# A one-core attention and feed-forward kernel: a new opening for stage one, another look at the weights' low bits, and inverse roots by Newton steps

## The reference

```python
x = x + LN(attention(LN(x)))     # q, k, v = LN(x) @ W + b; causal softmax((q k^T + bias) / sqrt(8)) v @ Wo + bo
x = x + LN(ffn(x))               # ffn is fed LN(x) too
# bias[i, j] = q_i . rel_key[clip(j - i + 255, 0, 255)]
# ffn: silu(x W1 s1) * (x W2 s2), then twice gelu(h H s), then (h W3) s3; W1, W2, H1, H2, W3 ternary, hidden width 512
```

## Time and profile before

| | |
|---|---|
| median of three runs | 788.54 us |
| the profiled execution: its own time, its span | 789.45 us, 787.7 us |
| PE, PE weight load, DVE, ACT, POOL busy | 646.7, 470.4, 565.0, 562.4, 301.0 us |
| mean granted TensorE clock | 0.927 |
| first matmul of stage two, first of stage three | 137.37, 577.69 us |
| packets of 16 engines, moved | 41169, 52.79 MB |

### The profile page before, as it was taken

How to read it: one execution, slowest core, us unless ns; L and a number is a source line. 1 busy time by engine, 2 the same in 40 slices (tenths; PEclk the granted TensorE clock), 3 DMA queues, 4 the chain that set the end, 5 groups by cost and what they waited for, 6 DMA issues and landing times. The chain is left out here.

```text
span 787.7 us, 19097 instructions
## 1 busy us (share of the span) xinstructions
PE 646.7 (82%) x8064; PEld 470.4 (60%) x8064; DVE 565.0 (72%) x927; ACT 562.4 (71%) x657; POOL 301.0 (38%) x190
## 2 busy tenths in 40 slices
PE   0667632679999999999999999987779899898993
PEld 0323310556767667676676766855568678687682
...
DMA packets 41169, 52.79 MB, mean 67 GB/s; under 512 B 7410, under 2 KB 31554, under 8 KB 38658
## 3 DMA queue, kind: packets, MB, share of 16 engines
...
...
## 5 line engine op out<-in xcount | busy, mean ns | idle before, releaser
L960 PE MATMUL p_s<-q_sb,k_sb 96*128 96x128 bf16 (+1 forms) x1600 | 170.8, 249 | 18.7 <-DVE probs L1106 14.9
L1224 ACT ACTIVATE probs<-p_s 128x1024 f32<-128x1024 f32 x160 | 156.8, 1018 | 17.8 <-DVE p_s L1115 10.8
L1224 ACT ACTIVATE probs<-probs 128x1024 f32<-128x1024 f32 x128 | 133.7, 1057 | 46.4 <-DVE probs L1106 46.2
L1004 PE MATMUL p_o<-probs,v_sb 128*32 128x128 f32 (+1 forms) x3200 | 159.1, 330 | 7.6 <-ACT o_acc L1242 5.3
L960 PEld LDWEIGHTS p_s<-q_sb,k_sb 96*128 96x128 bf16 x1600 | 112.7, 100 | 77.7 <-issue 29.0
L916 POOL TENSOR_SCALAR_AFFINE_SELECT even_b<-even_b 128x2048 f32<-128x2048 f32 x32 | 75.5, 2360 | 216.3 <-ACT even_b L1235 216.3
L1106 DVE TENSOR_TENSOR probs<-p_s,even_b 128x1024 f32<-128x1024 f32 x96 | 115.0, 1220 | 28.4 <-PE p_s L960 16.0
L1004 PEld LDWEIGHTS p_o<-probs,v_sb 128*32 128x32 f32 x3200 | 84.5, 111 | 40.7 <-issue 13.5
L1653 PE MATMUL p_z<-hid_hi,h_hi 128*128 128x512 f32 x256 | 102.3, 399 | 1.7 <-POOL hid_lo L1574 1.7
L1656 PE MATMUL p_z<-hid_lo,h_hi 128*128 128x512 f32 x256 | 100.8, 394 | 0.0
L981 PE MATMUL p_s<-q_rows,rel_w 72*128 72x64 bf16 x2048 | 84.8, 197 | 18.2 <-DVE probs L1106 8.7
...
## 6 DMA issues: line engine op xcount, KB each, us to landing
...
q_dram<-q_parts SPq DMA_DIRECT2D x12, 256.0 KB, 3.5
k_dram<-k_parts SPq DMA_DIRECT2D x12, 256.0 KB, 3.8
qr_dram<-q_turned SPq DMA_DIRECT2D x12, 256.0 KB, 3.5
...
every<-in_L_ffn_h_w_dram SPq DMA_DIRECT2D x2, 1024.0 KB, 8.3
```

Of the source, the lines that this page charges most:

```text
L960: last = nc.tensor.matmul(slot[:, c:c + n * BLK], k_sb[hg][:, h * S + j * BLK:h * S + (j + 1) * BLK], ap(q_sb[hg], at, [[HG * S, KROWS], [ ...
L1004: last = nc.tensor.matmul(p_o[32 * h:32 * h + 32, at:at + blocks * BLK], v_sb[hg][:, j, h * 32:(h + 1) * 32], probs[n % PBUFS][:, h, col * ...
L1224: nc.scalar.activation(to, got, ACT.Exp, scale=SCALE).then_inc(t_exp, 1)
```

## The change

Six things change. (1) SP loads the bias table as it lies (`rel_n`) and PE transposes it into `p_v`; the other small loads count on semaphores of their own, the three weights on `s_wts`; `kb_c` is computed behind the table's parts, and the wait for `g_ext` (`s_gld`) stands in the first batch. (2) GpSimd no longer fills the padding rows of `q_sb` and `k_sb`; it fills a tile `pads`, and SP copies that by four transfers, waits for them, and then loads the weights. (3) The root of batch 1 stands behind `kf` of batch 0 on ACT. (4) The look at the weights is three passes of ACT over the low 16 bits of each word, all at the end of the first batch; GpSimd has no part in it. (5) All inverse roots past stage one are Newton steps on DVE, in place of ACT's Sqrt and DVE's reciprocal. (6) In the last unit the outputs and the projection stand two steps earlier, DVE's `first_again` one, and GpSimd does the scaling of both norms.

```diff
+def inverse_root(nc, dve, x, room, done, at):
+    bits = mybir.dt.int32
+    t, y = room[:, :, 0], room[:, :, 1]
+    nc.vector.tensor_scalar(t.bitcast(bits), x[:, :].bitcast(bits), 1, None, ALU.logical_shift_right).then_inc(done, 1)
+    dve.wait_ge(done, at + 1)
+    nc.vector.tensor_scalar(y.bitcast(bits), t.bitcast(bits), -1.0, float(ROOT_GUESS), ALU.mult,
+                            ALU.add).then_inc(done, 1)
+    for i in range(ROOT_STEPS):
+        dve.wait_ge(done, at + 2 + 3 * i)
+        nc.vector.scalar_tensor_tensor(out=t, in0=y, scalar=-0.5, in1=x[:, :], op0=ALU.mult,
+                                       op1=ALU.mult).then_inc(done, 1)
+        dve.wait_ge(done, at + 3 + 3 * i)
+        nc.vector.tensor_tensor(t, t, y, ALU.mult).then_inc(done, 1)
+        dve.wait_ge(done, at + 4 + 3 * i)
+        nc.vector.scalar_tensor_tensor(out=y, in0=t, scalar=1.5, in1=y, op0=ALU.add,
+                                       op1=ALU.mult).then_inc(done, 1)
 def normalised(nc, dve, ffn, n, which, src):
 
-    at = n * PRE + 6 + 5 * which
-    dve.wait_ge(ffn.r_sd, n * 2 + which + 1)
-    nc.vector.reciprocal(ffn.rs[:, :], ffn.rs[:, :]).then_inc(ffn.r_dv, 1)
-    dve.wait_ge(ffn.r_dv, at)
+    at = (2 * n + which) * ROOT_OPS
+    inverse_root(nc, dve, ffn.rs, ffn.st, ffn.r_root, at)
+    dve.wait_ge(ffn.r_root, at + ROOT_OPS)
     for t in range(NB):
-        last = nc.vector.tensor_scalar(ffn.y[:, t, :], src[:, t, :], ffn.mv[:, t, 0:1], ffn.rs[:, t:t + 1],
+        last = nc.vector.tensor_scalar(ffn.y[:, t, :], src[:, t, :], ffn.mv[:, t, 0:1], ffn.st[:, t, 1:2],
                                        ALU.subtract, ALU.mult)
-    last.then_inc(ffn.r_dv, 1)
+    last.then_inc(ffn.r_dv, 2)
 
...
-                             (bq_c[:, :], bq.rearrange("(p a) -> p a", a=1)),
+            sp.dma_start(rel_n[:, :, :], ap(rel.tensor, 0, [[HD, 128], [128 * HD, P // 128], [1, HD]])).then_inc(s_relt, 16)
+            for dst, src in ((wq_sb[:, :], Wq), (wk_sb[:, :], Wk), (wv_sb[:, :], Wv)):
+                sp.dma_start(dst, src).then_inc(s_wts, 16)
+            for dst, src in ((bq_c[:, :], bq.rearrange("(p a) -> p a", a=1)),
                              (bk_c[:, :], bk.rearrange("(p a) -> p a", a=1)),
                              (r0_c[:, :], ap(rel.tensor, 0, [[0, H], [1, HD], [1, 1]])),
-                             (bv_b[:, :, :], ap(bv.tensor, 0, [[0, 128], [0, NB], [1, 128]])),
-                             (rel_t[:, :], ap(rel.tensor, 0, [[1, HD], [HD, P]]))):
+                             (bv_b[:, :, :], ap(bv.tensor, 0, [[0, 128], [0, NB], [1, 128]]))):
                 sp.dma_start(dst, src).then_inc(s_par, 16)
             sp.wait_ge(s_xin, 16)
             tokens(1)
...
+            sp.wait_ge(s_pool, 9)
+            for p in range(2):
+                for rows, dst, which in ((ROWS + PARTS, q_sb[p], 0), (ROWS, k_sb[p], 1)):
+                    n = KROWS - rows
+                    sp.dma_start(ap(dst, rows * (HG * S), [[HG * S, n], [512, HG * S // 512], [1, 512]]),
+                                 ap(pads, which * 512, [[2 * 512, n], [0, HG * S // 512], [1, 512]])).then_inc(s_pads, 16)
+            sp.wait_ge(s_pads, 16 * 4)
...
+            nc.gpsimd.memset(pads[:, 0, :], 0.0)
+            step(nc.gpsimd.memset(pads[:, 1, :], 1.0), 9)
             for p in range(2):
-                step(nc.gpsimd.memset(q_sb[p][64:KROWS, :], 0.0), 9 + 4 * p)
-                step(nc.gpsimd.memset(k_sb[p][64:KROWS, :], 1.0), 10 + 4 * p)
                 pad = v_sb[p][:, :, :].rearrange("p n (h d) -> p n h d", h=HG)
...
-                if b == 0:
-                    remainder(0)
-                    remainder(1)
-            remainder(2)
...
                 dve.wait_ge(s_kx, b * KX + 2)
+                if first:
+                    dve.wait_ge(s_gld, 16)
                 nc.vector.tensor_tensor(k_ext[:, :], k_ext[:, :], g_ext[:, 0:2], ALU.add).then_inc(s_kx, 1)
...
             layernorm(0, True)
-            dve.wait_ge(s_par, 8 * 16)
-            nc.vector.tensor_tensor(kb_c[:, :], bk_c[:, :], r0_c[:, :], ALU.add).then_inc(s_gs, 1)
-            nc.vector.tensor_scalar(rel_s[:, :], rel_t[:, :], rel_t[:, 0:1], None, ALU.subtract).then_inc(s_gs, 1)
+            rel_t = p_v[0:HD, 0:P]
+            dve.wait_ge(s_gtr, 1)
+            nc.vector.tensor_copy(gx[:, 2:3], rel_t[:, 0:1]).then_inc(s_gs, 1)
+            dve.wait_ge(s_gs, 1)
+            nc.vector.tensor_scalar(rel_s[:, :], rel_t, gx[:, 2:3], None, ALU.subtract).then_inc(s_gs, 1)
             dve.wait_ge(s_gs, 2)
...
-            dve.wait_ge(s_gld, 16)
+            dve.wait_ge(s_par, 4 * 16)
+            nc.vector.tensor_tensor(kb_c[:, :], bk_c[:, :], r0_c[:, :], ALU.add).then_inc(s_gs, 1)
...
-            def rounded(i):
+            def low_bits(i):
                 act.wait_ge(s_every, 16 * len(WEIGHTS))
-                if i >= 2:
-                    act.wait_ge(s_wabs, i - 1)
-                got, part = checked(i)
-                nc.scalar.activation(part, got, ACT.Copy).then_inc(s_whi, 1)
-            def largest(i):
-                act.wait_ge(s_wlo, i + 1)
-                _, part = checked(i)
-                nc.scalar.activation(part, part.bitcast(F32), ACT.Abs, accum_out=low_max[:, i:i + 1]).then_inc(s_wabs, 1)
+                if i > 0:
+                    act.wait_ge(s_wabs, i)
+                n = every.shape[1]
+                c = slice(i * (HC * HID), min((i + 1) * (HC * HID), n))
+                low = every[:, c].bitcast(mybir.dt.uint16).rearrange("p (c two) -> p c two", two=2)[:, :, 0]
+                nc.scalar.activation(low_part[:, 0:c.stop - c.start], low, ACT.Copy,
+                                     accum_out=low_max[:, i:i + 1]).then_inc(s_wabs, 1)
 
             def batch(b, first, last_batch):
-                if last_batch:
-                    largest(0)
-                    rounded(2)
-                    largest(1)
-                if not last_batch:
+                if not first and not last_batch:
                     root(b + 1)
...
+                if first:
+                    root(1)
...
-                    rounded(0)
-                    rounded(1)
+                    for i in range(CHECKS):
+                        low_bits(i)
 
             root(0)
             transposed(0, True)
-            act.wait_ge(s_par, 8 * 16)
-            act.wait_ge(s_gs, 1)
+            act.wait_ge(s_par, 4 * 16)
+            act.wait_ge(s_gs, 10)
             batches(act, batch)
-            largest(2)
...
+            pe.wait_ge(s_relt, 16)
+            for x in range(P // 128):
+                last = nc.tensor.transpose(p_v[0:HD, x * 128:(x + 1) * 128], rel_n[:, x, :], ident[:, :])
+            last.then_inc(s_gtr, 1)
             transposes(0, True)
-            pe.wait_ge(s_par, 8 * 16)
+            pe.wait_ge(s_wts, 3 * 16)
             project_qk(0, True)
+            pe.wait_ge(s_gs, 2)
             project_v(0, True)
-            pe.wait_ge(s_gs, 10)
+            pe.wait_ge(s_gs, 11)
...
-    FFN_AT = {17: OUTPUTS, 20: PROJECT, 32: HIDDEN, STEPS: 3, STEPS + 1: 4, STEPS + 2: 5}
+    FFN_AT = {15: OUTPUTS, 18: PROJECT, 32: HIDDEN, STEPS: 3, STEPS + 1: 4, STEPS + 2: 5}
     PARTS_OF = {3: [(0, 0, 1), (1, 0, 1)], 4: [(2, 0, 2)], 5: [(2, 2, 2)]}
-    ROOT_AT = {22: 0, 29: 1}
-    FIRST_AT = {21: 0, 23: 1, 28: 2, 30: 3}
+    FIRST_AT = {19: 0, 27: 1}
...
+            def scaled(which, src, steps):
+                pool.wait_ge(ffn.r_root, (which + 1) * ROOT_OPS)
+                pool.wait_ge(ffn.r_dv, 5 + 5 * which)
+                for t in range(NB):
+                    last = nc.gpsimd.tensor_scalar(ffn.y[:, t, :], src[:, t, :], ffn.mv[:, t, 0:1], ffn.st[:, t, 1:2],
+                                                   ALU.subtract, ALU.mult)
+                last.then_inc(ffn.r_dv, steps)
+            scaled(0, ffn.y, 2)
             pool.wait_ge(ffn.r_dv, 7)
             pool.wait_ge(ffn.r_x, 16)
             nc.gpsimd.tensor_tensor(ffn.x1_first[:, :, :], ffn.x1_first[:, :, :], ffn.y[:, :, :], ALU.add).then_inc(ffn.r_x1, 1)
+            scaled(1, ffn.x1_first, 2)
...
+                dve.wait_ge(ffn.r_dv, 5)
+                inverse_root(nc, dve, ffn.rs, ffn.st, ffn.r_root, 0)
 
             def first_again():
                 dve.wait_ge(ffn.r_x1, 1)
                 statistics(nc, dve, ffn.st, ffn.mv, ffn.rs, lambda t: ffn.x1_first[:, t, :], ffn.r_dv, 8, ffn.alone)
+                dve.wait_ge(ffn.r_dv, 10)
+                inverse_root(nc, dve, ffn.rs, ffn.st, ffn.r_root, ROOT_OPS)
 
             def first(k):
                 if k in FIRST_AT:
-                    (first_y, first_scale, first_again, first_hidden)[FIRST_AT[k]]()
+                    (first_y, first_again)[FIRST_AT[k]]()
...
-            def pre_root(n, which):
-                act.wait_ge(r_dv, n * PRE + (5, 10)[which])
-                nc.scalar.activation(ffn.rs[:, :], ffn.rs[:, :], ACT.Sqrt).then_inc(r_sd, 1)
-            def post_root(n):
```

(50 more changed lines are left out.)

20 lines of the change are left out of this document (4 added, 16 removed).

## The result

The changed kernel takes 798.87 us (median of 4 runs, 797.51 to 800.71), the kernel before on the same chip 788.63 (788.49 to 789.47): a ratio of 1.013, 95% interval 1.0115 to 1.0146. It is 10.2 us slower where 13.7 faster was forecast. The profiled executions span 797.8 and 787.7 us, 10.1 apart.

What follows compares the result with a forecast made beforehand. Stage one was taken as a chain of small steps with gaps, feed-forward turns as bound by TensorE with DVE nearly gapless. Terms -22.8 (stage one), -2.0 (last unit), +11.1 (turns) gave -13.7: 774.8 us against 788.54, range 770 to 779.

Steps and rivals of the forecast that it cites:

- Opening: Stage one up to batch 0's k_ext: 12.7 us gained; ends 14, or 8 if the small loads land late.
- Look at the weights: Stage one, batch 0 to 1: three ACT passes, 2.0 us gained; ends 3.5 gained and 3 lost.
- About 40.5, and ACT wants them at 39.9. I charge 0.5: Look at the weights: their landing about 40.5 against ACT's need at 39.9, charged 0.5 us.
- Rival C: Weights or wide-stride pass hold ACT, by pads' landing or passes of 11.8: 5.5 us more, 780.3; chance 0.14.
- Last batch and end: Last batch to the end of stage one: 8.1 us gained; ends 5.3 and 11.2.
- Last unit: Last attention unit, Newton chains for ACT's roots: about 2.0 us gained; ends 5 gained and 1 lost.
- The first of them ... 2.8 gained: Last unit: first ACT root leaves the chain to o_acc, where TensorE waits 4.24; 2.8 us gained.
- I take 2.8: Last unit: GpSimd's scaling of 8 operations, taken as 2.8 us; ends 1.0 and 4.
- Stage three: Feed-forward turns with Newton chains: 11.1 us lost (0, 3.6, 3.6, 3.9 by turn); ends 8 and 17.
- the sign I gave for the turn's end: Turns 1 and 2: TensorE idle again about 4 us on DVE act_f, where it read 1.09.
- rival D: TensorE's granted clock falls behind stalls of 3 to 4 us: 4 us more, 778.8; chance 0.10.
- Rivals A and B: A: Newton steps cost far more, 796 at 0.45 us each, chance 0.04. B: DVE has more air, 767.6, chance 0.14.

Runs made afterwards that it cites:

- e3: Changed kernel with bv_b's load on its own semaphore, issued behind the second batch's tokens; 797.94 us.
- e10: Changed kernel with bv_b loaded as 128 pieces in place of 1024 and read eight times by the value add; 793.77 us.
- e2: Changed kernel with the weights' loads issued ahead of the four pad copies, the wait for pads only before the last batch; 791.25 us.
- e12: Changed kernel with later roots as in the kernel before, bv_b as 128 pieces, weights behind tokens, pads behind the first batch's stores; 769.16 us.
- e4: Changed kernel with the last unit's two scalings on VectorE behind their Newton chains, in place of GpSimd; 793.88 us.
- e6: Changed kernel with weights ahead of pads, bv_b's own late wait, Newton roots only in the last unit, its scalings on VectorE; 772.06 us.
- e8: Changed kernel with five Newton steps in place of three; 815.42 us.

## Why the prediction was wrong, point by point

**Opening, 12.7 forecast, 8.9 got.** Rightly seen: the memsets, rel_t, the root behind kf. What failed is "Ends: 14 ... 8 if the small loads land late": I took the late landing for an end where it was the case. bv_b stood in the same list before, hidden since everything waited for the 24.30 of rel_t. e3 shows 23.33, so the chain's own sum (24.4) was right but for this load, and 1 us too long.

**Look at the weights, 2.0 forecast; 5.7 of the opening's gain lost.** This is the step that failed worst: 7.7 us, a third of the miss. "About 40.5, and ACT wants them at 39.9. I charge 0.5" fell in "pads to 25, waits to about 28.5": SP issued the last pad at 31.3 and waited to 39.2. Of the 10.7 us by which the weights were issued late (39.2 for 28.5), 6.0 came with bv_b through the g_ext round trip (e10 issues them at 33.2), and most of the rest from the pads, which took 7.1 us to land, where I had used 3.5. The passes are as priced (1.91, 1.91, 1.48 and 0.19 each); by these rows neither 16 bits nor the stride costs anything. Rival C had this mechanism at 5.5; e2 gives 6.9 to 7.7 for it. Yet this step alone didn't turn the sign: e2, without it, is still at 791.25.

**Last batch and end, 8.1 forecast.** From k_ext(1) to stage two the old kernel took 72.4 (64.99 to 137.37), the new 69.0: 3.4 gained. Up to k_ext(3) the 5.3 forecast for DVE's chain came (5.4: 108.74 to 100.14, less the 3.2 from before); behind it 2.0 were lost, where 2.8 more were forecast. GpSimd's part of the look is gone, but ScalarE now waits 4.5 for k_dram and 5.1 for m_dram, the stores I had named as the next limit and priced as nearly free. e12, with these waits at 4.3 and 6.2, shows that they stay when all before them is early. No run moves these stores, so that they are the whole of the 2.0 is argued, not shown.

**Last unit, 2.0 gain forecast, 4.2 lost.** "The first of them ... 2.8 gained" came as 1.4: the wait fell by 2.9, but "project and outputs two steps earlier have their inputs" was wrong by 0.61 and 1.00. "I take 2.8" for the scaling was 6.2, beyond my upper end of 4: the row I was nearest to is one instruction of 1024 elements, where this is eight with two per-partition scalars. o_acc and y are late by that: y's transposes start 63.1 us after o_rcp, before 59.0, which is the 4.2. With VectorE's 2.14 in its place (e4, e6) 1.3 to 1.4 are still lost: in none of the orders tried was there a gain to have by a chain on this engine.

**Stage three, 11.1 forecast, 12.4 lost.** Right that the chains are on the path, and the total is near, but in part by luck: it is made up otherwise. Newton operations were 0.21 apart (0.205 taken). Counted between p_post's first transposes, turn 0 cost 1.3 (I had 0; e8 shows both its chains on the path), turn 1 4.5 (3.6), turns 2 and 3 6.7 (7.5). In turn 1 y's transposes were late by about what I had said (2.9 for 3.1), but the sign I gave for the turn's end, TensorE idle for about 4 us on DVE's act_f, didn't show: that wait was 1.17 in turn 1 (1.09 before) and 0.98 in turn 2. Of turn 1's 4.5 only 1.7 are idle time; 2.8 are TensorE's busy time, 49.3 in place of 46.5 us for the same work. That is rival D, the clock, of which I had taken nothing into the sum: the chains' waits alone came to less than I had priced, and the clock made up the difference; two rows of the changed kernel's windows, where the one before stood at 1.00:

```profile
659.00:676.00 17.00, 14.29 (x61) 11.63 (x60) 16.16 (x72) 10.03 (x17) 2.40 (x1) 0.92 0.00 0
676.00:691.50 15.50, 13.35 (x48) 9.71 (x47) 10.53 (x28) 7.64 (x12) 8.50 (x10) 0.87 0.00 1
```

The sum: of the miss, 16.2 us (3.8, 7.7 and 4.7 by the three parts) lie in stage one, 6.2 in the last unit, 1.3 in stage three. Rivals A and B fell (0.21 a step; no air on VectorE). The sign was mine to lose: a sure loss of 11 us was set against a gain of 22.8 that hung on three unmeasured landings.
